# Between the first and the second layer of a four-layer graph network: projection, two norms and the table's store rearranged, and one sum moved from Pool to DVE

## The reference, cut to what matters

```python
h = relu(layernorm(x))
x = x + L0(h, ...)        # typed attention over the edges
h = relu(layernorm(x))
x = x + L1(h)             # degree-normalised sum over the edges
h = relu(layernorm(x)); x = x + L2(h, edge_attr)   # gated sum
h = relu(layernorm(x)); x = x + L3(h)              # mean, two products, norm, gelu

def L0(x, ...):           # its tail; x here is h above
    h_agg = segment_sum(m * attn, dst)           # 8 heads of 16 features
    h = typed_linear(h_agg, ntype, Wa)           # 3 node types
    alpha = sigmoid(skip)[ntype]
    h = layer_norm(h * alpha + x * (1 - alpha), ln_g, ln_b)
    h = h + x
    return gamma * h + beta                      # gamma, beta: FiLM rows
```

## Time and profile before

| what | value |
| --- | --- |
| median of 3 runs | 5103.66 us (5099.78 to 5104.33) |
| the profiled execution | 5097.74 us, its span 5095.7 us |
| busy share: PE / PEld / DVE / ACT / POOL | 60 / 50 / 61 / 30 / 68 % |
| mean granted TensorE clock | 0.714 of full speed |
| the chain that ended last | POOL 43%, issue 20%, DMA 14%, DVE 10%, PE 6%, ACT 3% |

### The profile page before, as it was taken

How to read it: one execution, slowest core, us unless ns; L and a number is a source line. 1 busy time by engine, 2 the same in 40 slices (tenths; PEclk the granted TensorE clock), 3 DMA queues, 4 the chain that set the end, 5 groups by cost and what they waited for, 6 DMA issues and landing times.

```text
span 5095.7 us, 77996 instructions
## 1 busy us (share of the span) xinstructions
PE 3039.8 (60%) x15683; PEld 2545.5 (50%) x15684; DVE 3111.3 (61%) x8258; ACT 1533.7 (30%) x2906; POOL 3443.9 (68%) x3594
## 2 busy tenths in 40 slices
PE   1845565656563444455555899999997444444443
PEld 1535455555453444444443677777775334343443
DVE  7447777777787666644554677777775444444443
ACT  3123233333313000001111566666664122222222
POOL 2477777777600777777774777777775777777775
PEclk9957777777767555557776999999998555555555
DMA  2267877778830221222224666666666222222224
GB/s 50 74 185 208 230 228 229 231 226 229 218 82 22 58 53 53 53 57 66 66 66 49 186 188 186 185 187 187 188 186 126 52 56 56 56 56 56 56 56 42
DMA packets 536502, 616.07 MB, mean 121 GB/s; under 512 B 97972, under 2 KB 420575, under 8 KB 536320
## 3 DMA queue, kind: packets, MB, share of 16 engines
q0 software_dynamic: 142176, 349.02, 26.7%
q1 hardware_dynamic: 394144, 265.13, 19.0%
HBM read 529.54 MB, written 84.25 MB: 120 GB/s over the span
## 4 chain that ended last, share of the span: by engine, by line
POOL 43%; issue 20%; DMA 14%; DVE 10%; PE 6%; ACT 3%; DVEq 2%; SPq 1%; POOLq 0%; ACTq 0%
POOL G L644 43%; DMA G<-tab,SRC 9%; DMA mvd<-G 3%; DVE ACCR L1379 3%; PE PB L490 2%; PE PSA L871 1%; PE PB L1061 1%; DVEq L603 1%; DVE ACCR L1828 1%; PE PB L483 1%; DVE ACCR L1386 1%; DVE FLG L1810 1%; DMA SCR<-in_ea_t 1%; ACT PB L1225 0%; PE PB L999 0%
## 5 line engine op out<-in xcount | busy, mean ns | idle before, releaser
L644 POOL DMA_INDIRECT G<-tab,SRC x3520 | 3357.1, 954 | 1424.0 <-issue 1036.4
L1379 DVE TENSOR_TENSOR ACCR<-ACCR,PSA 128x128 f32 (+2 forms) x3536 | 1126.5, 319 | 745.8 <-PE PSA L871 387.2
L871 PE MATMUL PSA<-G,S 128*128 128x128 f32 x3520 | 861.7, 422 | 1155.5 <-DMA G<-tab,SRC 982.5
L871 PEld LDWEIGHTS PSA<-G,S 128*128 128x128 f32 x3520 | 739.8, 311 | 1266.3 <-DVE ACCR L1379 699.2
L1362 DVE TENSOR_TENSOR S<-PB,REL 128x512 f32<-128x512 f32 x884 | 606.1, 686 | 38.5 <-DVE ACCR L1828 10.1
L999 PE MATMUL PB<-QTR,ST 128*128 x1792 | 345.7, 354 | 293.2 <-ACT ST L1188 148.5
L999 PEld LDWEIGHTS PB<-QTR,ST 128*128 128x128 f32 x1792 | 303.5, 255 | 328.9 <-issue 327.4
L871 PE MATMUL PSA<-FLG,S 128*128 128x256 f32 x1760 | 424.2, 385 | 2.1 <-DVE FLG L1810 1.8
L871 PEld LDWEIGHTS PSA<-FLG,S 128*128 128x128 f32 x1760 | 338.6, 193 | 148.0 <-issue 88.1
L871 PE MATMUL PSA<-SCR,S 128*128 128x137 f32 x1792 | 336.3, 346 | 14.9 <-DVE ACCR L1379 14.9
L871 PEld LDWEIGHTS PSA<-SCR,S 128*128 128x128 f32 x1792 | 312.7, 252 | 19.7 <-DVE SCR L1724 19.7
(11 more groups left out here) (311 smaller groups left out, 3795.0 us busy)
## 6 DMA issues: line engine op xcount, KB each, us to landing
mvd<-G SPq DMA_DIRECT2D x224, 256.0 KB, 3.3
MV<-mvd SPq DMA_DIRECT2D x224, 256.0 KB
G<-tab,SRC POOLq DMA_INDIRECT x3520, 2.5
SCR<-in_ea_t SPq DMA_DIRECT2D x880, 64.0 KB
S<-relt SPq DMA_DIRECT2D x224, 128.0 KB, 4.9
SCR<-reld SPq DMA_DIRECT2D x220, 128.0 KB
tab<-SCR SPq DMA_DIRECT2D x57, 128.0 KB, 1.8
tab<-G SPq DMA_DIRECT2D x50, 128.0 KB, 1.7
```

What stands on the lines that cost most here:

```text
L644: nc.gpsimd.indirect_dma_start(out=rows[:, slot, j, :], out_offset=None, in_=table, in_offset=bass.IndirectOffsetOnAxis(ap=SRC[:, k:k + 1] ...
L871: last = nc.tensor.matmul((PSA if banks is None else banks)[:, par, j, 0:width], S[:, slot, j, :], rhs(j), start=True, stop=True)
L1379: v_.tensor_tensor(rows, rows, banks[:, par, j, 0:width], ALU.add).then_inc(s["rows_added"], 1)
```

## The change

The first layer's preparation, the part between the layers and one number in layer 2 are touched. In words:

- Between the layers, the eight operations that scale the sums head by head go; the inverse sums are taken into a compact tile `INV`, multiplied into the type masks (`WEIGHT`, 50 x 3 x 8 columns), and the masking multiply of the projection uses these. The degree's inverse root (now `ALPHA2`) is taken ahead of the projection.
- The moments of the projection's output are taken in the projection's loop, two steps behind the take-out, instead of in one row behind it.
- In the norms, ACT takes (21, 30, 21) of the 50 blocks instead of 30 each time. In the middle one DVE applies the affine row, adds to `X` and takes the moments first for its own 20 blocks, then waits for ACT and does the other 30.
- The table's store is three DMAs: blocks 0 to 9 once ACT has scaled them, blocks 21 to 49 when DVE is done, then blocks 10 to 20.
- The FiLM sum leaves Pool. DVE does it in iteration 1 of layer 0 (quads 6 to 13), behind the quad's reduce, in 8 pieces of at most 7 blocks, with `MV` as scratch. Iteration 1 is written out for that.
- In the plan, 26 small operations become 4.
- In layer 2 SP stores turn t's block at step 4t + 11.

```diff
-PIECE = 5
+PIECE = 7
-            at_edge = {0, sz.iters, LAG - 1, LAG, last - 1, last} | ...
+            at_edge = {0, 1, sz.iters, LAG - 1, LAG, last - 1, last} | ...
-        ON_ACT = NS * 3 // 5
+        ON_ACT = (NS * 21 // 50, NS * 3 // 5, NS * 21 // 50)
+        NORMED = [sum(ON_ACT[:n]) for n in range(4)]
+        INV = ACCR[:, accw:accw + NS * HEADS].rearrange("p (b h) -> p b h", h=HEADS)
+        WEIGHT = ACCR[:, accw + NS * HEADS:...].rearrange("p (b t h) -> p b t h", t=TYPES, h=HEADS)
@@ dve_proj, step
+                if has_block(b) and n == 1:
+                    by_head = [P, TYPES, HEADS, DH]
+                    nc.vector.tensor_tensor(
+                        MB[:, r, :, :].rearrange("p t (h d) -> p t h d", h=HEADS),
+                        acc0[:, bass.ds(b, 1), 0:D].rearrange("p o (h d) -> p o h d", h=HEADS).to_broadcast(by_head),
+                        WEIGHT[:, bass.ds(b, 1), :, :].rearrange("p o t h -> p (o t) h").unsqueeze(3).to_broadcast(by_head),
+                        ALU.mult).then_inc(s["placed"], 1)
+                m = b - 4
+                if has_block(m) and n == 1:
+                    dve.wait_ge(s["evacuated"], m + 1)
+                    nc.vector.bn_stats(STATS[:, bass.ds(m, 1), :]..., QT[:, bass.ds(m, 1), :]...).then_inc(stats_taken, 1)
                 m, rm = b - 2, r
                 if has_block(m):
-            pairs(dve, step, 2)
+            pairs(dve, step, 2 if n == 0 else 4)
@@ Pool, ahead of the flags
-            pool.wait_ge(planned, FILM_KNOWN)
-            for b in range(0, NS, PIECE):
-                some = slice(b, b + PIECE)
-                piece = [P, PIECE, D]
-                each(acc1[:, some, :], H[:, some, :], bc(ROWS[:, 3, :], piece, 1), ALU.mult)
-                each(acc1[:, some, :], acc1[:, some, :], bc(ROWS[:, 2, :], piece, 1), ALU.add)
-                each(X[:, some, :], X[:, some, :], acc1[:, some, :], ALU.add)
@@ Pool, ahead of layer 1
-            pool.wait_ge(table_out, 16)
+            pool.wait_ge(table_out, 48)
@@ sp_edge_rows
-                due_now = turn_at(i, u, 8)
+                due_now = turn_at(i, u, 10)
-            steps(sp, step, after(8), 2)
+            steps(sp, step, after(10), 2)
@@ SP, between the layers
-            sp.wait_ge(table_made, 1)
-            sp.dma_start(tab1.rearrange("(b p) d -> p b d", p=P), H[:, :, :]).then_inc(table_out, 16)
+            table, half_act = tab1.rearrange("(b p) d -> p b d", p=P), ON_ACT[2] // 2
+            for some in (slice(0, half_act), slice(ON_ACT[2], NS), slice(half_act, ON_ACT[2])):
+                if some.stop == NS:
+                    sp.wait_ge(table_made, 1)
+                else:
+                    sp.wait_ge(normed, NORMED[2] + some.stop)
+                sp.dma_start(table[:, some, :], H[:, some, :]).then_inc(table_out, 16)
@@ ACT
             layer0_steps(act, step, exponentials)
+            root(ALPHA2)
             act_proj(act, 1)
             normalise(QT, QT, ACT.Identity)
-            root(ALPHA)
             normalise(X, H, ACT.Relu)
@@ DVE, plan
-            for m in range(1, PARTS):
-                c(v_.tensor_scalar(off, grp, float(m * sz.chunk), float((GROUP - 1) * sz.chunk), ALU.is_ge, ALU.mult))
-                c(v_.tensor_tensor(tpos, tpos, off, ALU.add))
+            c(v_.tensor_copy(partI, grp))
+            c(v_.tensor_scalar(partI, partI, sz.chunk.bit_length() - 1, None, ALU.logical_shift_right))
+            c(v_.tensor_copy(off, partI))
+            c(v_.scalar_tensor_tensor(tpos, off, float((GROUP - 1) * sz.chunk), tpos, ALU.mult, ALU.add))
@@ DVE, layer 0
+            def film(u):
+                some = slice(u * PIECE, min((u + 1) * PIECE, NS))
+                wide = [P, some.stop - some.start, D]
+                part = MV[:, :, :, :].rearrange("p r j d -> p (r j) d")[:, 0:wide[1], :]
+                c(v_.tensor_tensor(part, H[:, some, :], bc(ROWS[:, 3, :], wide, 1), ALU.mult))
+                c(v_.tensor_tensor(part, part, bc(ROWS[:, 2, :], wide, 1), ALU.add))
+                c(v_.tensor_tensor(X[:, some, :], X[:, some, :], part, ALU.add))
@@ DVE, layer 0's step, at its end
+                if isinstance(i, int) and i == 1 and u * PIECE < NS:
+                    film(u)
@@ DVE, between the layers
-            probs = acc0[:, :, D:D + HEADS]
-            c(v_.tensor_scalar(probs, probs, 0.5, None, ALU.max))
-            c(v_.reciprocal(probs, probs))
-            for h in range(HEADS):
-                c(v_.tensor_tensor(acc0[:, :, h * DH:(h + 1) * DH], acc0[:, :, h * DH:(h + 1) * DH],
-                                   acc0[:, :, D + h:D + h + 1].to_broadcast([P, NS, DH]), ALU.mult))
+            c(v_.tensor_scalar(ALPHA2[:, :], DEG[:, :], 1.0, 1.0, ALU.add, ALU.max))
+            root(ALPHA2)
+            c(v_.tensor_scalar(INV, acc0[:, :, D:D + HEADS], 0.5, None, ALU.max))
+            c(v_.reciprocal(INV, INV))
+            c(v_.tensor_tensor(WEIGHT, MASK[:, :, :].unsqueeze(3).to_broadcast([P, NS, TYPES, HEADS]),
+                               bc(INV, [P, NS, TYPES, HEADS], 2), ALU.mult))
             dve.wait_ge(w_next, 16)
             dve_proj(dve, 1)
-            c(v_.tensor_copy(IOTAP, iota[:, :]))
-            layer_norm(QT, QT, relu=False)
-            c(v_.tensor_tensor(QT, QT, vec(1), ALU.mult))
-            c(v_.tensor_tensor(X[:, :, :], X[:, :, :], QT, ALU.add))
-            c(v_.tensor_scalar(ALPHA[:, :], DEG[:, :], 1.0, 1.0, ALU.add, ALU.max))
-            root(ALPHA)
-            layer_norm(X, H, by=ALPHA)
-            dve.sem_inc(table_made, 1)
+            spread()
+            normalise(QT, QT, False)
+            for some in (slice(ON_ACT[1], NS), slice(0, ON_ACT[1])):
+                if some.start == 0:
+                    dve.wait_ge(normed, NORMED[2])
+                wide = [P, some.stop - some.start, D]
+                c(v_.tensor_tensor(QT[:, some, :], QT[:, some, :], bc(ROWS[:, 1, :], wide, 1), ALU.mult))
+                c(v_.tensor_tensor(X[:, some, :], X[:, some, :], QT[:, some, :], ALU.add))
+                moments(X, range(some.start, some.stop))
+            spread(by=ALPHA2)
+            normalise(X, H)
+            dve.sem_inc(table_made, 1)
+            c(v_.tensor_copy(IOTAP, iota[:, :]))
+            dve.wait_ge(normed, NORMED[3])
```

More of the change, by code:

```diff
@@ L117, in build @@
         ALPHA = sb("ALPHA", [P, NS])
+        ALPHA2 = sb("ALPHA2", [P, NS])
         DEG = sb("DEG", [P, NS])
@@ L1380, in row_adder, with moments, spread @@
                 return add
-            def layer_norm(src, dst, relu=True, by=None):
-                for b in range(NS):
+            def moments(src, blocks):
+                for b in blocks:
                     v_.bn_stats(STATS[:, b, :], src[:, b, :]).then_inc(stats_taken, 1)
+            def spread(by=None):
                 norms[0] += 1
@@ L1576, in _ @@
             dve.wait_ge(x_loaded, 16)
-            layer_norm(X, H)
+            moments(X, range(NS))
+            spread()
+            normalise(X, H)
+            dve.wait_ge(normed, NORMED[1])
             dve.wait_ge(windows_in, 32 * NC)
```

34 lines of the change are left out of this document (16 added, 18 removed).

## The result

The changed kernel takes 5075.23 us (median of 5 runs, 5070.88 to 5077.58), the kernel before 5103.66 beside it (5 runs, 5098.45 to 5106.71): ratio 0.9943, 95% interval 0.9932 to 0.9953. That is 28.4 us less; the forecast was 34.7 less (5069, range 5057 to 5087). Two of the three chips on which the experiments ran take 6.3 to 6.4 ms for either kernel, because the engines wait longer inside the layers there: between 300 and 1400 us Pool waits 308 us for DVE's multiply (L1740) in `after_again`, and 36 in the changed kernel's first profile. Why is open. Outside the layers, and in the length of single instructions, their traces agree with the others to some 0.7 us, so of those runs mainly such stretches are read.

A forecast was written before the change was run, and what follows sets the result against it. Pool's gathers were taken to bound the layers; outside them every step on the chain counted. Gains of 25.8 us between the layers and 8.9 in the front made 34.7, set against the median 5103.66: 5069 us, range 5057 to 5087.

The forecast's parts named there:

- the loop: Second projection between the layers: moving the moments into its loop gains 9.0 us, 9.5 less 0.5 for longer passes.
- FiLM: Sum moved from Pool to DVE: costs nothing in layer 0's iteration 1, gains 2.5 us in the first projection.
- the front: Stretch before the first gather: plan, first norm and FiLM off Pool together gain 8.9 us.
- The head scaling: Between the layers, ahead of the second projection: eight scaling operations replaced by one multiply into WEIGHT, gain 5.4 us.
- the middle norm: Between the layers, behind the second projection: blocks divided anew between ACT and DVE, gain 7.3 us.
- the last norm with its store: End of the stretch between the layers: norm gains 1.9 us, split table store 2.2, together 4.1.
- The plan's 4.5: Before the first gather, DVE's 26 small operations become four: gain 4.5 us.
- The first norm: Before the first gather, ACT's 30 blocks (11.65 us) give way to DVE's 29 (9.8) as the limit: gain 1.9.
- first rival: Second projection: each bn_stats lengthens it by 0.195 us, 9.8 instead of 0.5, so 5078; chance 0.12.
- The second rival: Layer 0, iteration 1: DVE's FiLM operations hold Pool's gathers, up to 24.7 us, so 5094; chance 0.04.
- The store at step 4t + 11: Layer 2, SP's queue: the later store lands 2 to 3 us before ACT needs it, so costs nothing.
- the slower case: Layer 2: SP's store lands too late for ACT and delays some 50 turns, 5220 at 8 us landing; chance 0.03.

The follow-up runs named there:

- `after_again`: The changed kernel without any edit, run again on another chip: 6311.42 us, ratio 0.9959 to the kernel before.
- `moments_row`: Against the changed kernel, the second projection's bn_stats in one row behind its loop, new masks kept: 6387.55 us, ratio 0.9977 to the kernel before.
- `loop_written_out`: Against the changed kernel, DVE's 50 blocks of the second projection as straight code with constant addresses: 6351.42 us, ratio 0.9925 to the kernel before.
- `after_third`: The changed kernel unaltered, run again on a chip that behaves as the first: 5076.40 us, ratio 0.9947 to the kernel before.

## Why the prediction was right, and where it was off

*Right in the range, the direction and most terms.* Of 34.7 us 28.4 came. No errors cancelled to bring it there: the loop fell short by 3.1, FiLM cost 2.4 and the front gave 1.1 less, and these make up the difference of 6.3 but for 0.3. The head scaling (5.4, came 5.7), the middle norm (7.3, came 7.1) and the last norm with its store (4.1, came 4.1, its split alone 2.2 as reckoned) are right with their mechanisms. The part of a store that does not shrink with its size was put at 1.6; the two rows (12.89 for 3200 KB, 1.7 for 128 KB) give 1.2, which changes the term by 0.1. The plan's 4.5 came in full: the first of its 350-element operations, at 53.24 in the earlier trace rows, starts at 48.76. The first norm gave 2.0 for 1.9. In the first projection every mask takes 0.55 now; beside Pool's FiLM they took up to 1.9, which is what the uneven take-outs of the earlier trace rows came from.

*The step that failed in the loop:* "The masking multiply keeps its 384 elements and, I assume, its 0.55". It keeps its 0.55; what grew is the idle piece ahead of it, from the loop's branch to the mask, by 0.18. On 21 passes that is 3.8, and the term's error is 3.1. The prediction held the loop to be "as long as now within 1 us" from first mask to last take-out; it went from 67.1 to 70.8. Of the 0.18, the register operation for the new operand is 0.07 and 0.10 stands behind the branch for a reason that stays open. The forecast looked for the cost in the bn_stats, and so did its first rival, which put 9.8 on them; `moments_row` shows that they cost 1.1 at most, since DVE waited 0.74 for PE in each pass. The rival's reason, that the masks come later and PE starts later, was right for another cause. The place was there to be read: "issue" idle of 0.19 ahead of each first mask of a pass, which the prediction passed over because nothing was waited for in it. `loop_written_out` shows what the loop costs in all: 12.3 us of a projection of 71.

*The step that failed for FiLM:* "DVE's multiply of 0.69 stands beside Pool's gathers, which keep their 0.95". That multiply (L1717) reads G and PB, one input in SBUF and one in PSUM. The operation to look at was its neighbour L1724, with both inputs in SBUF. The trace of before has it beside a long gather; DVE's timeline and Pool's:

```profile
515.01 0.69 DVE L1724 TENSOR_TENSOR SCR<-MV,SCR 128x512 f32<-128x512 f32 x1 [1.02 <-DMA MV<-mvd]
```

```profile
515.37 1.15 POOL L644 DMA_INDIRECT G<-tab,SRC  x1 [0.30 <-issue]
```

L1724 ends at 515.70 and the gather at 516.52, once more 0.82 later. Of before's gathers 64 to 878 in layer 0, 110 are longer than 1.0 us, 29 us in sum above 0.945 each, and the changed kernel has 114 with as much. In before 77 of them end 0.80 to 0.83 after an L1724, and the other 33 end 0.74 to 0.77 after one of DVE's scans (L1653, L1660, L1675, L1678), which have both inputs in SBUF too. So it was there before the change. By the Trainium skill ("SBUF — State Buffer", "SBUF: two separate sides") an operation of DVE with two SBUF inputs takes the port pair that it shares with GpSimd, but only against GpSimd work that reads SBUF, and the other waits for the whole instruction. The trace agrees, once a gather counts as such work: its indices (SRC) lie in SBUF. That reading them is the part that is held is an inference; the traces show the hold and that PSUM operands end it. The prediction had the rule and drew the opposite from it, taking a gather for work that reads no SBUF. The second rival's mechanism occurred, but not its 24.7: a gather is held only if it begins while such an operation runs, and only for what is left of it, so 7 or 8 gathers of 32 lost 0.1 to 0.9 each. The rival had a chance of 0.04, so this cost was missed, though it was small.

*The front* was expected to give 8.9; it gave 7.8 and, in `after_third`, 9.3. In the first profile the last plan store took 21.1 to land (issued at 105.27, SP goes on at 126.35) against 19.24, and 19.0 in the other. The stores themselves were issued 6.5 earlier in both, as forecast (6.4). FiLM's part was put at 2.5 and measured at 3.1; 6.5 and 3.1 less the 1.8 of the landing are the 7.8.

*The store at step 4t + 11* cost nothing, as forecast, and the slower case didn't occur: ACT's block goes on waiting for DVE.

*The rest of layer 0.* The prediction said that it is wrong "if a layer's own length changes by over 3 us". By the profiles layer 0 did, from 1158.3 to 1165.9 between its first and last gather, and 1168.9 in `after_third`. 2.4 and 4.4 of that are the held gathers; the rest is the spread of single executions told above, which is wider than the sign allowed for, as far as the profiles can tell. The forecast had no term for it; that the profiled execution of before was a fast one of its kind had been allowed for in setting the forecast against the median, and that was right: the median of 5075.2 lies 6 above 5069 and 12 above the 5063 that the profile alone would have given.

## What to carry to other kernels

Look at "issue" idle in a short loop as you look at a wait: where an engine's block has only three or four short operations, the branch and the address arithmetic are a real part of it (here 12 of 71 us together), and a new operand on the path can cost more than a new operation beside it. Ask of each operation that is moved beside indirect gathers of Pool how many of its inputs lie in SBUF; an operand in PSUM took the whole cost away at the same length. And before a term is set to nothing because a neighbour does no harm, make sure that the neighbour has the same kinds of operands.

## What the runs showed of the hardware that was not expected

A gather held by a DVE operation with two SBUF inputs ended 0.81 to 0.83 us after that operation's end in all 15 long gathers of iteration 1 in the profiles of the changed kernel and of `after_third`. The shortest distance from the operation's start to a held gather's is 0.05 (289.98 and 289.93). A gather that begins only 0.01 after it (284.10 and 284.09 in `after_third`) keeps its 0.95, and the DVE operation takes 1.14 instead of 1.09: there the gather came first. Two blocks of a projection with the same DVE operations take 2.81 or 2.21 us, by whether they stand in a loop, with branch and computed addresses, or are written out. Behind the branch of that loop the next instruction starts 0.13 us later in two programs and 0.23 in the others. The same kernels take 5.1 ms in the first and the last measurement and 6.3 on two other chips, with an undisturbed gather as long as here (0.95); what stops the engines inside the layers there is open.
